# Expert feed-forward: left-over tokens in the second half, second product of the first half with activations stationary, first expert begun half by half

## The reference, cut to what matters

```python
capacity = max(1, int(Sz * CAP_FACTOR / E) + 1)            # 257
scores = softmax(x @ router_w.T)                            # per token, over 8 experts
gate_vals, sel_idx = top_k(scores_t, capacity)              # per sequence and expert
tokens = x[b_idx, sel_idx]                                  # 2 x 8 x 257 rows of 256
h = gelu(einsum('becd,edh->bech', tokens, w1) + b1)         # 1024 wide
y = einsum('bech,ehd->becd', h, w2) + b2
out = zeros.at[b_idx, sel_idx].add(y * gate_vals[..., None])
```

## Time and profile before

| | us |
|---|---|
| median of the 3 runs | 837.75 |
| lowest, highest | 835.34, 842.58 |
| span of the profiled execution (first to last instruction) | 832.3 |
| median less that span | 5.45 |

### The profile page before, as it was taken

The page is one execution under the profiler, slowest core; times in us unless marked ns, Lnnn a source line. Parts: engine busy times, 40 slices in busy tenths (PEclk is TensorE's granted clock), DMA queues, the critical chain, the costliest instruction groups (busy, mean ns, idle before and its releaser), DMA issues.

```text
span 832.3 us, 12982 instructions
## 1 busy us (share of the span) xinstructions
PE 766.2 (92%) x4971; PEld 627.0 (75%) x4971; DVE 534.6 (64%) x1148; ACT 396.6 (48%) x694; POOL 303.0 (36%) x275
## 2 busy tenths in 40 slices
PE   7899889999999999999999989984689999999996
PEld 7765546756656555579979888883689999999996
DVE  7777784576676684266454589985747755666551
ACT  3555443464455334564381345433035765557561
POOL 5511002100211023047371142334335767666673
PEclk9999999999999999999999999996899999999999
DMA  7000000000000100010021201120212445444532
GB/s 184 2 1 0 1 0 1 1 1 1 0 1 1 52 2 1 7 45 3 2 61 37 102 1 52 51 76 27 102 32 71 134 108 147 133 90 104 139 38 27
DMA packets 20359, 38.28 MB, mean 46 GB/s; under 512 B 4786, under 2 KB 15754, under 8 KB 17994
## 3 DMA queue, kind: packets, MB, share of 16 engines
q1 hardware_dynamic: 13641, 29.02, 10.7%
q0 software_dynamic: 6656, 8.43, 6.0%
HBM read 28.91 MB, written 8.40 MB: 45 GB/s over the span
## 4 chain that ended last, share of the span: by engine, by line
PE 60%; DVE 16%; ACT 4%; issue 3%; POOL 2%; DMA 0%; ACTq 0%; DVEq 0%
PE ps L464 19%; PE ps L1148 12%; PE ps L626 9%; PE ps L730 5%; PE ps L647 2%; PE ps L648 2%; PE ps L588 2%; DVE rep L1743 1%; DVE sm L1544 1%; DVE Pb L1548 1%; PE ps L1088 1%; PE ps L1076 1%; DVE sm L1553 1%; PE ps L563 1%; PE ps L798 1%
## 5 line engine op out<-in xcount | busy, mean ns | idle before, releaser
L626 PE MATMUL ps<-PT,VA 128*65 128x512 f32 (+1 forms) x288 | 147.5, 594 | 1.7 <-ACT PT L2035 1.3
L2035 ACT ACTIVATE PT<-ps 128x512 f32<-128x512 f32 x128 | 75.7, 592 | 63.4 <-PE ps L648 63.4
L1148 PE MATMUL ps<-he,wh 128*128 128x258 f32 x768 | 104.1, 288 | 0.0
L464 PE MATMUL ps<-GT,wh 128*128 128x258 f32 x768 | 96.4, 284 | 0.4 <-DVE GT L1841 0.4
L1148 PEld LDWEIGHTS ps<-he,wh 128*128 128x128 f32 x768 | 95.4, 189 | 0.4
L464 PEld LDWEIGHTS ps<-GT,wh 128*128 128x128 f32 x768 | 93.3, 189 | 0.6 <-issue 0.6
L2634 POOL DMA_INDIRECT out_dram<-ye,idx x40 | 64.1, 1603 | 22.6 <-DVE ye L1853 12.0
L1871 DVE TENSOR_TENSOR he<-het,he 128x516 fp32r<-128x516 f32 x64 | 44.6, 697 | 41.4 <-ACT he L1899 40.8
L2388 POOL TENSOR_TENSOR ssq<-ssq,half 128x8 f32<-128x8 f32 x16 | 26.1, 1638 | 122.6 <-DVE ssq L1269 122.6
L647 PE MATMUL ps<-QA,KA 128*128 128x512 f32 x144 | 68.5, 476 | 0.4 <-ACT QB L1899 0.4
L588 PE MATMUL ps<-KA,QA 128*128 128x368 f32 x192 | 59.7, 418 | 3.8 <-DVE x L1353 2.9
(11 more groups left out here) (286 smaller groups left out, 1556.0 us busy)
## 6 DMA issues: line engine op xcount, KB each, us to landing
wr<-in_w1e_dram SPq DMA_DIRECT2D x8, 1024.0 KB, 4.9
wr<-in_w2e_dram SPq DMA_DIRECT2D x8, 1024.0 KB, 4.8
x<-in_x_dram SPq DMA_DIRECT2D x4, 512.0 KB, 6.7
w<-in_w_dram SPq DMA_DIRECT2D x2, 1024.0 KB, 5.0
y_dram<-yr SPq DMA_DIRECT2D x3, 512.0 KB, 3.0
out_dram<-x SPq DMA_DIRECT2D x3, 512.0 KB, 4.1
gt<-y_dram,idx POOLq DMA_INDIRECT x40, 3.3
out_dram<-ye,idx POOLq DMA_INDIRECT x40, 3.9
```

What stands on the lines that cost most here:

```text
L464: op = pe.matmul(o, l, r, start=n == 0, stop=n == len(calls) - 1)
L626: pe.matmul(bank[6 + hf][0:65, :], VA[b][0:K, kt, h, :], PT[u % 4][0:K, :], start=kt == 0, stop=kt == 8).then_inc(p_pv, 1)
L1148: op = pe.matmul(bank[dc][:, 0:258], w2h[i][:, wc_], he[j][:, m, 258 * c:258 * c + 258], start=n == 0, stop=n == 23)
L2035: a.activation(PT[u % 4][0:K, :], bank[4 + u % 2][0:K, :], ACT.Exp, bias=0.0 if K == 128 else mcol[:, b:b + 1]).then_inc(a_exp, 1)
```

## The change

- The left-over tile goes to the second half: the halves are now columns 0 to 255 (tiles 0, 1) and 256 to 513 (tiles 2, 3 and 4). The padding and its memsets go. The first half is gathered by two DMAs and not three, the second by three and not two.
- The first product's halves have 256 and 258 columns; they stand next to each other in PSUM, so that the Gelu reads 514 columns in one piece (516 before).
- The second product takes the second half first, as before with w2 stationary (`n_` 0 and 1). For the first half (`n_` 2 and 3) the activations `he` are stationary and w2 moves with 256 columns: `n_` 2 gives tile 0, `n_` 3 tile 1, as tokens x features. These need no transposes: `row_out` on DVE scales them straight out of PSUM and adds `gb2`, the bias times the gate, which POOL makes for each expert in `gated_row` from a row that SP fetches (`fetch_b2`). ACT's two bias activations for that half and PE's four transposes per expert go. `rows_out` in the middle of `n_` 2 now turns tiles 2, 3 and 4.
- `LEAVE` is the order of the scatters that follows from this.
- Expert 0: PE begins the first product for the first half of m = 0, 1, 2 (`AHEAD`) as soon as that half's tokens are there, ahead of turning the second half; m = 2 uses banks 0 and 1. The two groups of 12 and 8 `warm` transposes become one of 6.

```diff
-COLS = [(0, 128), (128, 128), (258, 128), (386, 128), (256, 2)]
+COLS = [(0, 128), (128, 128), (256, 128), (384, 128), (512, 2)]
+
+HALVES = [(0, 256), (256, 258)]
+
+GATHERED = ((0, (0, 1)), (1, (2, 3, 4)))
+
+AHEAD = 3
 
 ROUTE = [(0, 4), (4, 4), (8, 4), (12, 2), (14, 2)]
 
-LEAVE = (0, 1, 4, 2, 3)
+LEAVE = (2, 3, 4, 0, 1)
...
+        GT = [[s4(f"GT{i}{j}", [128, 2, 514], F32R) for j in range(2)] for i in range(2)]
...
-        yT = s4("yT", [128, 2, 516])
+        yT = s4("yT", [128, 2, 258])
+        b2r = [s4(f"b2r{i}", [128, D]) for i in range(2)]
+        gb2 = [s4(f"gb2{i}", [128, 2, D]) for i in range(2)]
...
+        def first_at(ex, m):
+
+            return 512 * (0 if ex == 0 and m == 2 else 4 + 2 * (m % 2)) + 256
...
-                for c, ss_ in ((0, (0, 1, 4)), (1, (2, 3))):
+                for c, ss_ in GATHERED:
...
             drain(index(0))
             warm(1, 46)
             rows = gathered(0)
-            for n in range(4):
-                if n == 2:
-                    warm(1, 12)
-                next(rows)
-            warm(1, 8)
+            next(rows)
+            next(rows)
+
+            def first_product(ex, m, c):
+                gT, at_ = GT[ex % 2], first_at(ex, m) + HALVES[c][0]
+                (c0, n_), bk = HALVES[c], at_ // 512
+                clear(bk)
+                w_ = [slice(1024 * k + 128 * m, 1024 * k + 128 * m + 128) for k in range(2)]
+                op = three(flat[:, at_:at_ + n_], [((wh1[0][:, w_[k]], wh1[1][:, w_[k]]),
+                                                    (gT[0][:, k, c0:c0 + n_], gT[1][:, k, c0:c0 + n_])) for k in range(2)])
+                busy[bk] = (a_g, 32 + 8 * ex + m + 1)
+                return op
+
+            pe.wait_ge(a_wh, 1)
+            pe.wait_ge(g_wh, 1)
+            warm(1, 6)
+            pe.wait_ge(v_gT, 2)
+            for m in range(AHEAD):
+                first_product(0, m, 0)
+            next(rows)
+            next(rows)
             second = index(1, 4, 0)
             for _ in range(4):
                 next(second)
             for ex in range(NE):
                 side_ = both(gathered(ex + 1) if ex + 1 < NE else idle(0), index(ex + 2) if ex + 2 < NE else idle(0))
-                gT = GT[ex % 2]
-                if ex == 0:
-                    pe.wait_ge(a_wh, 1)
-                    pe.wait_ge(g_wh, 1)
-                    pe.wait_ge(g_gz, 1)
...
                 for m in range(8):
-                    for c in range(2):
-                        bk, cs = 4 + 2 * (m % 2) + c, slice(258 * c, 258 * c + 258)
-                        clear(bk)
-                        w_ = [slice(1024 * k + 128 * m, 1024 * k + 128 * m + 128) for k in range(2)]
-                        op = three(bank[bk][:, 0:258], [((wh1[0][:, w_[k]], wh1[1][:, w_[k]]), (gT[0][:, k, cs], gT[1][:, k, cs]))
-                                                        for k in range(2)])
-                        busy[bk] = (a_g, 32 + 8 * ex + m + 1)
-                    op.then_inc(p_h, 1)
+                    if ex or m >= AHEAD:
+                        first_product(ex, m, 0)
+                    first_product(ex, m, 1).then_inc(p_h, 1)
                     next(second, None)
-                    if ex and m == 0:
-                        pe.wait_ge(a_yT, 4 * ex)
...
                 for n_ in range(4):
-                    c, dc = divmod(n_, 2)
+                    dc = n_ % 2
                     clear(dc)
                     calls = [(m, j, i) for m in range(8) for j, i in ((1, 0), (0, 1), (0, 0))]
                     for n, (m, j, i) in enumerate(calls):
                         if n_ == 0 and n % 3 == 0:
                             pe.wait_ge(v_he, 8 * ex + m + 1)
-                        wc_ = slice(256 * m + 128 * dc, 256 * m + 128 * dc + 128)
-                        op = pe.matmul(bank[dc][:, 0:258], w2h[i][:, wc_], he[j][:, m, 258 * c:258 * c + 258],
-                                       start=n == 0, stop=n == 23)
+                        if n_ < 2:
+                            wc_ = slice(256 * m + 128 * dc, 256 * m + 128 * dc + 128)
+                            op = pe.matmul(bank[dc][:, 0:258], w2h[i][:, wc_], he[j][:, m, 256:514], start=n == 0, stop=n == 23)
+                        else:
+                            c0 = COLS[n_ - 2][0]
+                            op = pe.matmul(bank[dc][:, 0:256], he[j][:, m, c0:c0 + 128], w2h[i][:, 256 * m:256 * m + 256],
+                                           start=n == 0, stop=n == 23)
                         if n % 6 == 5:
                             next(side_, None)
                         if n_ == 2 and n == 11:
-                            pe.wait_ge(a_yT, 4 * ex + 2)
-                            rows_out(ex, 0, ((6, (0, 1)), (7, (4,))))
+                            pe.wait_ge(a_yT, 2 * ex + 2)
+                            rows_out(ex, 0, ((6, (2, 3)), (7, (4,))))
                     op.then_inc(p_y, 1)
-                    busy[dc] = (a_yT, 4 * ex + n_ + 1)
+                    busy[dc] = (a_yT, 2 * ex + n_ + 1) if n_ < 2 else (v_ye, 5 * ex + n_ + 2)
                 drain(side_)
-            pe.wait_ge(a_yT, 4 * NE)
-            rows_out(NE - 1, 3, ((0, (2, 3)),))
...
+            def row_out(ex, s):
+
+                v.wait_ge(p_y, 16 + 4 * ex + s + 3)
+                v.wait_ge(g_con, 6 + ex + 1)
+                v.scalar_tensor_tensor(ye[ex % 2][:, s, :], bank[s][:, 0:256], gate[:, ex, s:s + 1], gb2[ex % 2][:, s, :],
+                                       ALU.mult, ALU.add).then_inc(v_ye, 1)
...
                 for m in range(8):
-                    if ex and m == 1:
-                        rows_out(ex - 1, ((0, (2, 3)),))
...
                     if n_ == 2:
-                        rows_out(ex, ((6, (0, 1)), (7, (4,))))
+                        rows_out(ex, ((6, (2, 3)), (7, (4,))))
                     next(side_, None)
                     next(side_, None)
+                row_out(ex, 0)
                 drain(side_)
                 if ex + 1 < NE:
                     w2n, c = wh2[(ex + 1) % 2], slice(1024, 2048)
                     v.wait_ge(a_wh, 2 + 6 * ex + 6)
                     v.tensor_tensor(w2n[1][:, c], wr[1][:, c], f(w2n[0][:, c]), ALU.subtract).then_inc(v_wh, 1)
-            rows_out(NE - 1, ((0, (2, 3)),))
+                row_out(ex, 1)
...
-                    bp = 4 + 2 * (m % 2)
-                    a.activation(het[m % 2][:, :].rearrange("p (c n) -> p c n", c=2), ps[:, bp:bp + 2, 0:258], ACT.Gelu,
-                                 bias=b1e[:, ex, m:m + 1]).then_inc(a_g, 1)
+                    at_ = first_at(ex, m)
+                    a.activation(het[m % 2][:, :], flat[:, at_:at_ + 514], ACT.Gelu, bias=b1e[:, ex, m:m + 1]).then_inc(a_g, 1)
...
+                    if s < 2:
+                        a.wait_ge(p_y, 16 + 4 * ex + s + 1)
+                        if ex and s == 0:
+                            a.wait_ge(p_yT, 2 * ex)
+                        a.activation(yT[:, s, :], bank[s][:, 0:258], ACT.Identity, bias=b2e[:, ex, s:s + 1]).then_inc(a_yT, 1)
...
-            for gT in (*GT[0], *GT[1]):
-                op = g_.memset(f(gT[:, :, 514:516]), 0.0)
-            op.then_inc(g_gz, 1)
...
+            def gated_row(ex):
+
+                g_.wait_ge(d_ln, 64 + 16 * (ex + 1))
+                if ex >= 2:
+                    g_.wait_ge(v_ye, 5 * (ex - 2) + 5)
+                g_.tensor_tensor(gb2[ex % 2][:, :, :], b2r[ex % 2][:, :].unsqueeze(1).to_broadcast([128, 2, D]),
+                                 gate[:, ex, 0:2].unsqueeze(2).to_broadcast([128, 2, D]), ALU.mult).then_inc(g_con, 1)
+
...
@@ -2643,6 +2670,7 @@
                 if ex:
                     scatter(ex - 1, 3)
                     scatter(ex - 1, 4)
+                gated_row(ex)
                 if ex + 1 < NE:
...
+            def fetch_b2(ex):
+                sp.dma_start(b2r[ex % 2][:, :], A["b2r"][ex].partition_broadcast(128)).then_inc(d_ln, 16)
...
             sp.wait_ge(p_rl, 5)
+            fetch_b2(0)
+            fetch_b2(1)
...
@@ -2767,6 +2800,8 @@
                     sp.wait_ge(g_wh, 2 + 3 * ex + 1)
                     sp.wait_ge(v_wh, 2 * ex + 1)
                     fetch_w(ex + 2, 0)
+                    sp.wait_ge(g_con, 6 + ex + 1)
+                    fetch_b2(ex + 2)
                     sp.wait_ge(a_wh, 2 + 6 * ex + 6)
```

35 lines of the change are left out of this document (14 added, 21 removed).

## The result

The changed kernel takes **832.47 us** (median of 11 runs, 829.58 to 837.12); the kernel before took 837.73 beside it (11 runs). The ratio is 0.9945, 95% interval 0.9924 to 0.9965: a gain of about 0.6% (833.1 was forecast), inside the 1% that I called no change. A later set of 12 runs of the same kernel gave 833.29 against 836.74 (ratio 0.9971, 0.9944 to 0.9997). So the two sets show gains of 5.3 and 3.5 us, on either side of the forecast 4.6.

The account below looks back on a forecast made before the run. PE, busy for 92% of the span and without waits inside the experts, was taken to bound the kernel. Gains of 2.9 + 0.3 + 1.0 + 0.4 = 4.6 us off 837.75 gave 833.1 us, range 829 to 838.5.

Parts of the forecast that it names:

- the 1% that I called no change: Outcome class for the whole kernel: a result within 1% (8.4 us) counts as same, given chance 0.89.
- Transposes: PE, behind slice 0 of each expert but the last: four transposes removed, 0.41 us each time, 2.9 us in all.
- Columns and roles: PE matmuls of both products: 256 columns instead of 258 save 0.3 us in all; activations stationary costs nothing.
- Steady expert: Experts in the middle of the kernel: time falls by 0.45 us, from 26.40 to 25.95 us.
- Start: Expert 0: its second product begins at 627.1 instead of 628.08, a gain of 1.0 us, between 0 and 1.65.
- rival 3: Expert 0's start: early half gives nothing because tables and gathers set the pace; 834.1 us; 77% together with the forecast.
- End: Kernel's tail: POOL's queue of scatters sets the pace, last scatter starts at 828.08 instead of 828.49, gain 0.4 us.
- "Nothing is added on PE: 0": Added POOL and DVE work in the experts: it does not reach PE, cost 0 us.
- Rival 1: Experts: POOL shuts out DVE's w2 subtraction, losing up to about 1 us in six experts; 839 us; 8%.
- Rival 2: Expert 0's start: granted clock falls, first 40 matmuls take twice as long, 4.9 us more; 838 us; 4%.
- a granted clock below 1 behind 612: Sign of a wrong forecast: PE's granted clock below 1 after 612 us, in expert 0's start.
- Distance from span to median: Whole kernel: the median's 5.45 us above the profiled span stays; span forecast 827.7, median 833.1 us.

Follow-up runs that it names:

- e3: Changed kernel with the four PE transposes put back behind slice 0 in experts 1 to 7, their result unused; 835.46 us, ratio 0.9984 to the kernel before.
- e4: Kernel before with only the second half's products cut from 258 to 256 columns; 836.41 us, ratio 0.9995 to the kernel before.
- e5: Changed kernel with w2 stationary and activations moving again in n_ 2 and 3; 833.16 us, ratio 0.9952 to the kernel before.
- e7: Changed kernel with expert 1's two index pieces one slice later on PE; 831.87 us, ratio 0.9948 to the kernel before.
- e2: Changed kernel without the early first half (AHEAD 0, warm-ups of 12 and 8 as before); 834.44 us, ratio 0.9957 to the kernel before.
- e1: Changed kernel with expert 7's gated_row moved into expert 6, behind POOL's two weight subtractions; 831.83 us, ratio 0.9935 to the kernel before.
- e6a: Changed kernel with one extra 512-element multiplication on POOL behind gated_row in experts 1 to 6; 831.66 us, one run.
- e6c: Changed kernel with four extra 512-element multiplications on POOL behind gated_row in experts 1 to 6, plus a POOL wait between second and third; 849.67 us, one run.
- e6b: Changed kernel with two extra 512-element multiplications on POOL behind gated_row in experts 1 to 6; 829.92 us, one run.
- e9: Changed kernel with PE's waits at the start of expert 0 filled by 9, 8 and 4 warm-ups; 832.0 us, ratio 0.9946 to the kernel before.
- e10: Changed kernel with e1's order, e7's index pieces and 9 and 8 warm-ups together; 830.15 us, ratio 0.9926 to the kernel before.

## Why the prediction was right, and where it was not

- **Transposes**, 0.41 us each: held (e3).
- **Columns and roles**, 0.3 us: e4 shows 0.3 for the columns, at the limit of what a trace can tell. An estimate by the Trainium skill, "TensorE: Matmul & The Clock Gate", section "Back-to-back issue gap", gives 0.8 ns for two columns; e4 shows about 0.35. The roles cost nothing, as forecast (e5).
- **Steady expert**, 25.95 forecast, 25.79 measured. The gain was 0.58 and not 0.45. The first product's 0.46 is the transposes' 0.41 and the columns' 0.05 to 0.07; of the second product's 0.12, 0.03 at most can be the roles, and the rest stays unexplained.
- **Start**, 1.0 forecast, 1.18 measured. The times of the steps came as reckoned, and e7 confirms that the first table set the pace. But I booked all of it to the early half, and e2, by one profile, shows that the early half earns 0.49 and the new order of gathers and halves 0.65. So rival 3, that the early half gives nothing, did not hold, but more of the gain than I thought would have come without it.
- **End**, 0.4 forecast, 0.33 measured, for the reason given: POOL's queue follows the transposes, and not the last product.
- **"Nothing is added on PE: 0"** is the step that failed. I had looked at the end of an expert alone, where `gated_row` stands beside weight work. In the last expert it starts in the middle of the slices and meets an `he1`: 0.89 us (e1). It cancelled what the steady experts gave in excess (0.14 x 6 = 0.8, a good part of it unexplained), so that the sum of 4.6 beside a measured 4.7 is in part luck.
- **Rival 1** is real but far off: the subtraction takes twice as long before PE notices. I put the point at 1.7 us of extra delay on DVE, 0.5 of play ahead of `he1` and 1.2 behind it. No run stands against it: two extras of POOL made `he1` 0.5 us late, 0.7 at most, with no wait of PE. With four POOL's own load comes in as well, so the exact point stays open. Its mechanism did strike, in expert 7 at another operation. The Trainium skill, "SBUF — State Buffer", section "Who interferes with whom", says that a DVE instruction with two inputs in SBUF and a GpSimd instruction that reads SBUF contend for a port pair that only one of them holds at a time; 695 to 2596 ns for one `he1` beside 1.63 us of POOL agrees in kind.
- **Rival 2**, 4% at 4.9 us, was mis-sized both ways; a granted clock below 1 behind 612 was one of my signs of being wrong. The clock fell in expert 0's first product in six profiles of versions with the early start (e1, e3, e5, e6a, e6c, and the second of the changed kernel), not in the first profile of the changed kernel, nor in e6b, e7, e9, e10, and not in the profiles of the three kernels without the early start (before, e2, e4). It cost 1.3 to 2.7 us where it fell, more than the start's whole gain. So in a part of the executions the early start loses time; the forecast span fits the profile in which it did not. That the waits of 0.4 to 0.9 us bring it on is likely and not shown: of eight profiles with all three waits two stayed clean, so that e9 and e10, filled and clean, could be chance.
- **Distance from span to median**: the 5.45 is 2 us plus the spread of executions. The forecast of the median subtracts the gain from a median and does not depend on it. The forecast of the span, 827.7, met 827.6 since the quick profile of before met a quick profile of after.
